# Loading the first group of three attention stages between the stores of their projections

## The reference

```python
x = x + _L0_attn_a_ref(_layernorm(x), ...)   # 16 heads, 8 key heads of width 32, scores capped by 50*tanh(./50)
x = x + _L0_ffn_ref(...)
x = x + _L0_attn_b_ref(_layernorm(x), ...)   # 16 heads, 4 key heads of width 16, plain softmax
x = x + _L0_ffn_ref(...)
x = x + _L1_attn_a_ref(_layernorm(x), ...)   # difference of two softmaxes, weighed by lambda, then a softmax again
...
q, k, v = x @ Wq, x @ Wk, x @ Wv; q, k = _rope(q), _rope(k)
energy = einsum('bqhad,bkhad->bahqk', qd, kd)
lam = exp(sum(lq1 * lk1)) - exp(sum(lq2 * lk2)) + LAM_INIT
diff = scores[:, 0] - lam * scores[:, 1]
```

## Time and profile before

| | us |
|---|---|
| median of 3 runs | 3083.19 (3069.79 to 3089.73) |
| profiled execution, its own time | 3076.73 |
| its span in the profile | 3075.0 |
| TensorE busy | 2478.8 (81%) |
| VectorE busy | 2081.9 (68%) |
| ScalarE busy | 1837.6 (60%) |
| GpSimd busy | 899.8 (29%) |
| mean DMA rate | 58 GB/s |

### The profile page before, as it was taken

The page is one execution under the profiler, slowest core; times in us unless marked ns, Lnnn a source line. Parts: engine busy times, 40 slices in busy tenths (PEclk is TensorE's granted clock), DMA queues, the critical chain, the costliest instruction groups (busy, mean ns, idle before and its releaser), DMA issues. The chain is left out here.

```text
span 3075.0 us, 68767 instructions
## 1 busy us (share of the span) xinstructions
PE 2478.8 (81%) x25192; PEld 1650.3 (54%) x25192; DVE 2081.9 (68%) x4873; ACT 1837.6 (60%) x3580; POOL 899.8 (29%) x971
## 2 busy tenths in 40 slices
PE   7788877878888698577677677776999786899998
PEld 3433326643333285334444344445888564788888
DVE  5288886667788467499899898995333344666652
ACT  2388974324445453288899898993222343576678
POOL 2223334120111232255455455550000122222223
PEclk9889988878999798799999999998999777898999
DMA  4523302253333212512211222004000476622210
GB/s 154 150 53 72 74 7 101 80 106 57 47 36 42 71 52 99 110 20 29 30 14 17 30 29 29 1 1 169 1 1 1 92 148 99 128 39 32 31 44 8
DMA packets 283033, 177.09 MB, mean 58 GB/s; under 512 B 205648, under 2 KB 242528, under 8 KB 280672
## 3 DMA queue, kind: packets, MB, share of 16 engines
q1 hardware_dynamic: 273552, 164.55, 26.0%
q10 hardware_dynamic: 9168, 8.41, 1.2%
HBM read 113.84 MB, written 54.66 MB: 55 GB/s over the span
## 5 line engine op out<-in xcount | busy, mean ns | idle before, releaser
L1297 ACT ACTIVATE ad_e<-ps,ad_nm 128x1024 f32<-128x1024 f32 (+7 forms) x512 | 384.0, 756 | 96.1 <-DVE ad_nm L1358 93.6
L1358 DVE TENSOR_REDUCE ad_nm<-ps 128x1 f32<-128x1024 f32 (+7 forms) x512 | 369.5, 749 | 54.5 <-PE ps L1228 54.0
L1331 POOL TENSOR_TENSOR ad_e<-ad_e,ad_c 128x128 f32<-128x128 f32 (+7 forms) x256 | 293.6, 1147 | 16.5 <-DVE ad_rz L1371 9.6
L1226 PE MATMUL ps<-ad_k_st,ad_q_st 96*128 96x512 bf16 (+3 forms) x768 | 212.7, 338 | 96.0 <-ACT ad_e L1297 52.1
L622 ACT ACTIVATE ab_e<-ps 128x512 f32<-128x512 f32 (+3 forms) x384 | 167.2, 490 | 205.3 <-PE ps L539 204.1
L375 PE MATMUL ps<-warm,ident_b 128*128 128x512 bf16 x512 | 157.6, 390 | 98.9 <-ACT ad_prT L1282 98.7
L1324 POOL TENSOR_TENSOR ad_e<-ad_e,later_k 128x128 f32<-128x128 f32 x256 | 119.2, 466 | 381.7 <-ACT ad_e L1297 381.7
L1382 DVE CUSTOM_DVE_ANT_0 ad_t<-ad_e,ad_rz 128x128 f32<-128x128 f32 (+7 forms) x256 | 223.7, 874 | 3.9 <-ACT ad_pr L1305 1.9
L1305 ACT ACTIVATE ad_pr<-ad_t,ad_low 128x128 f32<-128x128 f32 (+7 forms) x256 | 200.3, 783 | 0.0
L1241 PE MATMUL ps<-ident,ad_pr 128*128 128x128 f32 x1152 | 177.7, 283 | 26.1 <-ACT ad_pr L1305 26.1
L1241 PEld LDWEIGHTS ps<-ident,ad_pr 128*128 128x128 f32 x1152 | 142.3, 145 | 91.0 <-ACT ad_pr L1305 54.9
(11 more groups left out here) (389 smaller groups left out, 7083.5 us busy)
## 6 DMA issues: line engine op xcount, KB each, us to landing
scr_a<-pa_parts SPq DMA_DIRECT2D x24, 512.0 KB, 2.7
aa_q_st<-scr_a SPq DMA_DIRECT2D x24, 512.0 KB, 8.1
split<-f_split SPq DMA_DIRECT2D x16, 768.0 KB, 3.9
ad_q_st<-scr_d SPq DMA_DIRECT2D x48, 256.0 KB, 9.8
g_w<-split SPq DMA_DIRECT2D x8, 1536.0 KB, 18.0
scr_d<-pd_parts SPq DMA_DIRECT2D x20, 384.0 KB, 2.5
st_w_first<-split ACTq DMA_DIRECT2D x5, 1536.0 KB, 8.3
aa_k_st<-scr_a SPq DMA_DIRECT2D x24, 256.0 KB, 8.9
```

What stands on the lines that cost most here:

```text
L1226: last = pe.matmul(m.ps[:, bank, 0:n], q_st[:, b, 2 * h + s, t * P:(t + 1) * P], k_st[:, b, s, cc * QB:cc * QB + n], start=True, stop=True)
L1297: act.activation(e[:, u % EB, s, 0:L], src, ACT.Exp, bias=nm[:, u % EB, s:s + 1], accum_out=z[:, u % EB, s:s + 1]).then_inc(exped[s], 1)
L1331: pool.tensor_tensor(e[:, k, 1, 0:L], e[:, k, 1, 0:L], c[:, k:k + 1].to_broadcast([P, L]), ALU.mult).then_inc(mixed, 1)
L1358: dve.tensor_reduce(nm[:, u % EB, s:s + 1], src, AX.X, ALU.max, negate=True).then_inc(maxed[s], 1)
```

## The change

Classes `FirstGroup` and `FirstPair` own the buffers and semaphores of queries, keys, output weights and lambda rows. They are made ahead of the projection, which calls their `load` between its stores; the attention takes them over.

```diff
@@ project_rope
+    half = len(items) // 2
+    share = -(-first.count // half)
...
                              parts[:, n % PB, :, :].bitcast(F32) if two else parts[:, n % PB, :, :]).then_inc(stored[n % PB], 16)
+                if n == half:
+                    for par in range(PB):
+                        sp.wait_ge(stored[par], 16 * len(range(par, half, PB)))
+                if n >= half:
+                    for k in range((n - half) * share, min((n - half + 1) * share, first.count)):
+                        first.load(sp, k)
@@ FirstGroup (aa, ab)
+        self.count = self.per + (7 if plain else 1)
...
+    def load(self, sp, k):
+
+        n = k - (6 if self.plain else 0)
+        if n < 0:
+            self.stage_row_part(sp, 0, k)
+        elif n < self.per:
+            self.stage_part(sp, 0, n)
+        elif n == self.per:
+            sp.dma_start(self.wo[:], self.wo_d.rearrange("(j p) n -> p j n", p=P)).then_inc(self.wo_loaded, 16)
@@ attention
             if plain:
-                stage_rows(0)
                 stage_rows(1)
             for g in range(B * GB):
                 if g >= 2:
                     sp.wait_ge(weighed, (g - 1) * NS)
-                stage(g)
+                if g >= 1:
+                    for n in range(per):
+                        first.stage_part(sp, g, n)
+                sp.dma_start(v_st[:, par, :, :, :], v_sb[:, b * BT:(b + 1) * BT,
+                                                         j * kv_in_group:(j + 1) * kv_in_group, :]).then_inc(v_staged[par], 16)
@@ weigh
+                if s == 0:
+                    pe.wait_ge(v_staged[par], i * 16 + (g // 2 + 1) * 16)
@@ FirstPair (ad)
+    def load(self, sp, k):
+
+        if k < 6:
+            self.stage_part(sp, 0, k)
+        else:
+            self.load_lambda(sp, k - 6, ("lq1", "lk1", "lq2", "lk2")[k - 6])
@@ diff_attention
-            for n, name in enumerate(("lq1", "lk1", "lq2", "lk2")):
-                sp.dma_start(lv[:, n, :], a[name].partition_broadcast(P)).then_inc(lam_loaded, 16)
...
+                if g >= 1:
+                    for n in range(6):
+                        first.stage_part(sp, g, n)
+                sp.dma_start(v_st[:, b, :, :], v_sb[:, b * BT:(b + 1) * BT, j, :]).then_inc(v_staged[b], 16)
...
-                        pe.wait_ge(staged[b], (i + u // PER) * (16 * 13) + 16 * 13)
+                        pe.wait_ge(staged[b], (i + u // PER) * (16 * 12) + 16 * 12)
```

More of the change, by code:

```diff
@@ L45, in sb, with take_over @@
         return self.stack.enter_context(self.nc.sbuf_tensor(f"{self.tag}_{name}", shape, dt))
+    def take_over(self, other):
+        self.stack.push(other.stack)
+        self.sems += other.sems
     def close(self):
@@ L192, in norm_transpose, with project_rope @@
     ph.close()
-def project_rope(nc, m, tag, w_d, tiles, wv_d, kv, hd, vpad, cos_d, sin_d, scr, v_sb, two=False):
+def project_rope(nc, m, tag, w_d, tiles, wv_d, kv, hd, vpad, cos_d, sin_d, scr, v_sb, first, two=False):
     ph = Phase(nc, tag)
@@ L395, in attention @@
+def attention(nc, m, tag, v_sb, first, scale, softcap):
+    ph = Phase(nc, tag)
+    ph.take_over(first.ph)
+    plain, hd, kv_in_group, per = first.plain, first.hd, first.kv_in_group, first.per
+    rows, aug = per * hd, 3 if plain else 0
     ER = 4
-    wo = ph.sb("wo", [P, GB, C])
-    q_st = ph.sb("q_st", [rows + aug, 2, HG, T], kind)
-    k_st = ph.sb("k_st", [rows + aug, 2, kv_in_group, T], kind)
+    wo, q_st, k_st, wo_loaded, staged = first.wo, first.q_st, first.k_st, first.wo_loaded, first.staged
@@ L404, in attention @@
     if plain:
-        q_row = ph.sb("q_row", [rows, 2, HG, T], BF16)
-        k_row = ph.sb("k_row", [rows, 2, T], BF16)
+        q_row, k_row, row_staged = first.q_row, first.k_row, first.row_staged
         nm = ph.sb("nm", [P, 2, HG, BT])
@@ L429, in attention @@
     share = HG // kv_in_group
-    N_DMA, SPLIT = 2 * per + 1, 6
+    N_DMA, SPLIT = 2 * per, 6
     PIECES = 12
@@ L451, in _ @@
         def _(sp):
[L452 to L468, removed]
@@ L470, in stage_rows @@
             def stage_rows(g):
-                b, j, par = g // GB, g % GB, g % 2
-                tok = slice(b * T, (b + 1) * T)
                 for n in range(6):
[L475 to L480, removed]
+                    first.stage_row_part(sp, g, n)
@@ L1254, in run @@
                         wait(pe, out_copied, i, QUADS, u // HG)
+                        if t == 0:
+                            pe.wait_ge(v_staged[b], (i + u // PER) * 16 + 16)
                     for kb in range((t + 1) * part // 3, (t + 1) * (part + 1) // 3):
@@ L2450, in attn_softcap @@
         with nc.sbuf_tensor("v_a", [P, TILES, 8, 32], F32) as v_sb:
+            first = FirstGroup(nc, "fa", a["scr_a"], a["wo_a"], 32, 2, 512, plain=False)
             with nc.sbuf_tensor("xnT_a", [P, KC, TOK], F32) as m.xnT:
-                project_rope(nc, m, "pa", a["wqk_a"], 6, a["wv_a"], 8, 32, 32, a["cos_a"], a["sin_a"], a["scr_a"], v_sb, two=True)
-            attention(nc, m, "aa", a["scr_a"], v_sb, a["wo_a"], 32, 2, 512, 256.0 ** -0.5, 50.0)
+                project_rope(nc, m, "pa", a["wqk_a"], 6, a["wv_a"], 8, 32, 32, a["cos_a"], a["sin_a"], a["scr_a"], v_sb,
+                             first, two=True)
+            attention(nc, m, "aa", v_sb, first, 256.0 ** -0.5, 50.0)
     def ffn(tag, chunks):
```

95 lines of the change are left out of this document (65 added, 30 removed).

## The result

| | before | changed |
|---|---|---|
| median of 4 runs | 3086.4 (3069.79 to 3089.73) | 3032.01 (3013.72 to 3038.04) |
| ratio to before | | 0.9841 [0.9808, 0.9873] |
| profiled execution, its own time | 3076.73 | 3036.48 |
| its span | 3075.0 | 3034.7 |

The forecast was 3028, the range 3010 to 3048. By the ratio the change gains 1.6% (1.3 to 1.9%), 49 us of 3086.

A forecast was written before the change was run, and what follows sets the result against it. Barrier-chained blocks were taken as bound by TensorE's DMA waits at three attention starts; 16.7 + 1.0 + 9.4 + 24.5 = 51.6 us gave 3025.1 from the profiled execution, 3031.6 from the median; 3028 between them, range 3010 to 3048.

The forecast's parts named there:

- Start of `aa`: ScalarE's first tanh in `aa` comes 16.7 us earlier, its own table load being what is late next.
- Values in `aa`: Before the first weighing in `aa`, the new wait for the values' copy costs 0 to 2.8 us, taken as 0.
- the rival: The values come late at the first weighing in `aa`, costing 2.8 us, total 3031; chance 0.08.
- TensorE's clock in `aa`: Early in `aa`, a shorter stop keeps TensorE at 2.4 GHz, gaining 0 to 1.9 us, taken as 1.0.
- Start of `ab`: VectorE's first row maximum in `ab` comes 9.4 us earlier, GpSimd's three instructions being late next.
- Start of `ad`: VectorE's first maximum in `ad` comes 24.5 us earlier, the making of lambda on VectorE being late next.
- Loads between the stores at 0: Loads among the stores of the projections' second halves delay nobody, priced at 0; from above 31 us.
- Slacks: Time a store's landing may slip before ScalarE waits for it: 9.0 us in `pa`, 5.0 in `pb` and `pd`.
- backlogs: DMA work piled up by loads among stores: 5.6 us in `pa`, 2.2 at most (4.4 last store) `pb`, 1.8 `pd`.
- The first rival: Loads at half rate hold up the projections' stores: 7.2, 10.9 and 13 us, together 31, total 3059; chance 0.09.
- The slower rival: Late stores pause TensorE, its clock halves, second-half projection items cost 3.43 us more each: 127 us, total 3155; chance 0.03.

The follow-up runs named there:

- late_v: Changed kernel with the copy of the first values in `aa` issued behind the six loads of group 1; ratio to the kernel before 0.9846.
- the late four: Profiles with `aa`'s loads not early: kernel before, only `ab` early, only `ad` early, loads behind all stores; run of `aa` 309.1 to 311.8 us.
- repetitions: The changed kernel run twice more with no edit; 3018.55 and 3023.43 us, ratios to the kernel before 0.9807 and 0.9819.
- `aa` alone: Changed kernel with only `aa` loading early, `ab` and `ad` loading at their block's start again; ratio to the kernel before 0.9954.
- warm: Changed kernel with one more unread TensorE matmul at each pair of scores of `aa`'s three narrower diagonal tiles; ratio to the kernel before 0.9799.
- lump: Changed kernel with all first-group loads of a stage behind one store, at the second half's first item; ratio to the kernel before 0.9883.

## Why the prediction was right, and where it was off

*Start of `aa`: right.* 16.7 forecast, 16.7 measured; the table load ends last, as named.

*Values in `aa`: right.* Taken as 0, bounded by 2.8: the copy landed in 3.3 us with 8.4 to spend (121.66 to 130.04). Neither of the two rows it was priced by was near: the 5.0 us of `ab` too are those of a copy behind other loads, twelve of them, and the 3.3 is the first figure of a copy with nothing ahead. `late_v` shows the mechanism of the rival, at 6.6. That is more than the 2.8 of the rival, which had the copy issued with the block's start: the six loads ahead take SyncE 3.1 us to issue (122.65 to 125.72), and the 11 us to land come on top.

*TensorE's clock in `aa`: wrong.* "I take 1.0", from 0 to 1.9 as a gain. The step that failed is that the clock in `aa` was taken as a matter of the first 20 us, with 0 as the worst case. It rises and falls all through the block. The early starts without added matmuls or late values spent 44 to 81 us at 0.50 and ran 307.7 to 317.4, the late ones 54 to 66 and 309.1 to 311.8. Against 310.3, the mean of the late four, the changed kernel ran 7.1 longer in its profile and 1.2 longer in its repetitions. The 1.2 lies inside the spread of the late four, so the runs show no gain, and a loss in two profiles (317.4, and 317.0 for `aa` alone) whose cause is open; the lower bound should have been some -8. Nor did the first 20 us go as argued. The Trainium skill ("TensorE: Matmul & The Clock Gate", Part 1: The HAM clock gate) says that the default state is the slow one and that activity releases it; from this I had argued that a short stop leaves the clock alone. In the trace the clock was at 1.00 when the block began and fell to 0.50 at 124.2 us, for 13.7 us. In the 4.2 us ahead of that TensorE had been busy 1.4 us: first the stop of 1.9 us, then a few matmuls for which ScalarE set the pace. Which of the two brings the fall the runs do not separate: in `warm`, with the same stop, the clock fell too, at 125.0, but for 3.4 us. Why the stretches between the first groups are 17 us long in some profiles and 3 to 10 in others is open as well.

*Start of `ab`: right.* 9.4 and 9.4, 3.0 us behind the block's start, GpSimd last.

*Start of `ad`: right.* 24.5 forecast, 24.8 measured; lambda takes 1253.18 to 1255.42, 2.24 us as before.

*Loads between the stores at 0: right.* Slacks of 9.0, 5.0 and 5.0 against backlogs of 5.6, up to 4.4 and 1.8: the greatest landings should have been 2.7 more, 8.3, 7.1 and 4.5, and were 8.6, 6.9 and 4.9. The first rival, 31 us, needs loads at half the rate beside stores; the window of `pa` speaks against it, with 259 GB/s for loads and stores together at a share of 1.00, more than the 212 of the loads alone. `lump` shows the mechanism when the backlog passes the slack: stores land in up to 12.7, 9.7 and 13.1 us, and `pb` and `pd` lose 9.6 and 10.3. The Trainium skill ("DMA: Bandwidth & Descriptors", Queues, rings and completion order), cited beside that rival, states that each DMA engine takes descriptors in ring order. The landings agree, 2.7 us without loads ahead and up to 8.6 with them in the changed kernel, up to 13.1 in `lump`; what the rival left out was whether anyone waits for the store.

*The slower rival* (the stall drops TensorE's clock) had no stall to begin with; TensorE is busy 14.00 of 14 at 1.00 in the busiest window of `pa`. In `lump`, which has the stalls, its second half fails too. The clock did fall during the stalls, in `pb` at 634.4 us, where TensorE had stopped at 632.6, and in `pd` at 1248.8 for 6.8 us, where it had stopped at 1244.0. But `pd`'s last items still came 3.0 to 3.4 us apart, and the projections lost 9.6 and 10.3 us, less than their stalls of 11.9 and 13.2, and not 3.4 more per item.

*The total.* The sum without the clock was 50.6, the three starts gave 50.9. The forecast of 3028 lies 4 below the median, 5 and 9 above those of the repetitions. That it came so near is in part luck: the median of the kernel before alone moved from 3072.34 to 3086.4 between measurements, and the wrong clock term was small beside the three starts.

## What to carry to other kernels

When a block begins with loads of what the block ahead has stored, ask from when on their source is complete; if that is halfway, the loads belong between the stores of the second half, a few per item. Whether they are free is a subtraction: backlog by measured rates of loads and stores, against the time from the issue of a store to the moment somebody wants its buffer. Beyond it engines stall, and the stall is paid unless the engine that paces has work in hand (20 us for the lump in `pb` and `pd`, nothing in `pa`). Before counting the gain, name what is late next at the block's start (here 1.3, 3.0 and 2.3 us).

## What the runs showed of the hardware

The granted clock of TensorE falls to 1.2 GHz inside a block in which TensorE never stops for long: in the changed kernel it was at 1.00 from 185 to 200 us, with TensorE busy 10.69 of 15, and at 0.50 from 206 to 223. The length of these stretches differs between executions of the same program: 80.6 us of the run of `aa` in one profile of the changed kernel, 61.2 in the two others. Between the profiles at 53.9 and 80.6 us it goes with some 3 us of run per 10 us. DMA traffic in the same place does not bring it alone: `warm` was at 1.00 from 206 to 223 with a DMA share of 0.76.

A stop of 6 us on ScalarE between a projection's items cost nothing in one projection (`pa`), and 9.6 and 10.3 us were the price of 11.9 and 13.2 in the two others.

A copy within SBUF of 256 KB, issued with nothing ahead in SyncE's queue, landed in 3.3 us; behind six loads it took 11.

The narrow loads moved 212 GB/s alone, at a DMA share of 1.07; mixed with the stores of `pa` it was 259 GB/s at 1.00. The stores landed up to 8.6 us behind their issue instead of 2.9.
